# The squares of the queries in two bf16 halves: one more square on ScalarE and one subtraction on GpSimd, summed by TensorE as bf16

## The reference

```python
q = (layernorm(x) @ Wq).reshape(B, 100, 16, 128)
k = (ctx @ Wk).reshape(B, 361, 16, 128)
v = (ctx @ Wv).reshape(B, 361, 16, 128)
q = q * rsqrt(mean(square(q), -1) + 1e-5) * gq
k = k * rsqrt(mean(square(k), -1) + 1e-5) * gk
attn = softmax(einsum('bqhd,bkhd->bhqk', q, k) / sqrt(128), -1)
x = x + tanh(g_xattn) * (einsum('bhqk,bkhd->bqhd', attn, v).reshape(B, 100, 2048) @ Wo)
x = x + tanh(g_ffn) * ffn(layernorm(x))      # ternary weights, activations in 8 bits
```

## Time and profile before

| | |
|---|---|
| median of 3 runs | 2375.84 us (2372.43 to 2377.09) |
| the profiled execution | 2376.88 us, its span 2375.1 us |
| TensorE busy | 2225.2 us, 94% of the span |
| VectorE busy | 1842.7 us, 78% |
| ScalarE busy | 1615.7 us, 68% |
| GpSimd busy | 1283.2 us, 54% |
| granted clock, mean | 0.973 of full |

### The profile page before, as it was taken

The page is one execution under the profiler, slowest core; times in us unless marked ns, Lnnn a source line. Parts: engine busy times, 40 slices in busy tenths (PEclk is TensorE's granted clock), DMA queues, the critical chain, the costliest instruction groups (busy, mean ns, idle before and its releaser), DMA issues. The chain is left out here.

```text
span 2375.1 us, 45246 instructions
## 1 busy us (share of the span) xinstructions
PE 2225.2 (94%) x16338; PEld 1572.4 (66%) x16338; DVE 1842.7 (78%) x4138; ACT 1615.7 (68%) x3374; POOL 1283.2 (54%) x1632
## 2 busy tenths in 40 slices
PE   3599999999999999999999999999999999869999
PEld 1367776777777777777677767676767777534444
DVE  4577878787878787877877888787777877669997
ACT  3567676777777777766776767776767767536665
POOL 4365655565656566665766676766666655300000
PEclk8799999999999999999999999999999999989999
DMA  7456767676767666657676777677767765636655
GB/s 204 104 108 114 142 129 135 128 144 122 148 126 148 124 139 128 132 108 138 130 151 123 146 136 139 138 141 147 136 146 131 137 108 112 149 109 142 139 141 125
DMA packets 919312, 317.50 MB, mean 134 GB/s; under 512 B 864528, under 2 KB 882224, under 8 KB 918832
## 3 DMA queue, kind: packets, MB, share of 16 engines
q1 hardware_dynamic: 919088, 314.60, 65.5%
HBM read 82.09 MB, written 19.40 MB: 43 GB/s over the span
## 5 line engine op out<-in xcount | busy, mean ns | idle before, releaser
L1084 POOL TENSOR_TENSOR ksplit<-khat,ksplit 128x512 bf16<-128x512 f32 (+1 forms) x384 | 454.8, 1186 | 72.3 <-ACT ksplit L615 71.4
L825 DVE TENSOR_TENSOR khat<-keys_ps,krs 128x512 f32<-128x512 f32 (+1 forms) x384 | 263.5, 686 | 279.2 <-POOL krs L1078 278.9
L1078 POOL TENSOR_TENSOR krs<-kvar,minus_half 128x4 f32<-128x4 f32 (+1 forms) x384 | 387.6, 1009 | 32.0
L635 ACT ACTIVATE early<-score_ps,nbias,qrs 100x361 f32<-100x361 f32 x512 | 329.3, 648 | 83.6 <-DVE nbias L843 82.1
L1075 POOL TENSOR_SCALAR kvar<-kss 128x4 f32<-128x4 f32 (+1 forms) x384 | 88.1, 229 | 551.4 <-DVE kss L815 549.4
L620 ACT ACTIVATE ksq<-keys_ps 128x512 f32<-128x512 f32 (+1 forms) x384 | 228.5, 596 | 193.2 <-PE keys_ps L25 193.1
L644 ACT ACTIVATE psplit<-early,rden 100x361 bf16<-100x361 f32 x512 | 304.5, 595 | 61.5 <-DVE rden L849 60.6
L23 PE MATMUL keys_ps<-wk_split,ctxT 128*128 128x512 bf16 (+1 forms) x768 | 296.7, 386 | 38.0 <-DVE khat L825 31.4
L855 DVE SCALAR_TENSOR_TENSOR psplit<-early,rden,psplit 100x361 bf16<-100x361 f32 x512 | 321.8, 637 | 7.1 <-ACT psplit L644 3.3
L833 DVE TENSOR_REDUCE nmax<-score_ps 100x1 f32<-100x361 f32 x512 | 268.5, 525 | 55.8 <-PE score_ps L25 55.6
L615 ACT ACTIVATE ksplit<-khat 128x512 bf16<-128x512 f32 (+1 forms) x384 | 240.7, 627 | 99.7 <-DVE khat L825 86.4
(11 more groups left out here) (136 smaller groups left out, 5331.6 us busy)
## 6 DMA issues: line engine op xcount, KB each, us to landing
w_raw<-in_ffn SPq DMA_DIRECT2D x96, 256.0 KB, 3.3
ctx_raw<-in_ctx SPq DMA_DIRECT2D x31, 256.0 KB, 3.3
xin<-in_x SPq DMA_DIRECT2D x32, 200.0 KB
xres<-in_x SPq DMA_DIRECT2D x32, 200.0 KB
x_rows<-xres SPq DMA_DIRECT2D x32, 200.0 KB
xin<-x_rows SPq DMA_DIRECT2D x25, 256.0 KB, 2.8
xres<-x_rows SPq DMA_DIRECT2D x25, 256.0 KB, 2.9
out<-xres SPq DMA_DIRECT2D x25, 256.0 KB, 2.0
```

The source lines that it names most:

```text
L635: act.activation(prob[:, b, h, :], score_ps[h % 2][0:SQ, 0:SK], ACT.Exp, bias=nbias[:, b, h:h + 1], scale=qrs[:, v // 2 % 2, r:r + 1], acc ...
L825: dve.tensor_tensor(khat[0:KV[t], k, :].rearrange("p (h d) -> p h d", h=G), keys_ps[k][0:KV[t], :].rearrange("p (h d) -> p h d", h=G), rs, ...
L1078: pool.tensor_tensor(krs[0:KV[t], k, :], kvar[0:KV[t], k, :], minus_half[0:KV[t], 0:G], ALU.pow).then_inc(krs_done, 1)
L1084: pool.tensor_tensor(ksplit[0:KV[t], t, 1, :], khat[0:KV[t], (u + t) % 2, :], ksplit[0:KV[t], t, 0, :], ALU.subtract).then_inc(k_lo_done, 1)
```

## The change

`queries_square` now squares each 128x400 block twice from the same PSUM bank: into a float32 tile of half the size (`qsq`, one block), and as bf16 into the high part of `qsq_split`. A new function on GpSimd, `query_squares_lo`, subtracts the one from the other into the low part. As `qsq` holds one block, ScalarE's next square waits for GpSimd's subtraction. `query_squares` waits for GpSimd and makes two bf16 products for each sequence and head; the weights are 128 columns, of which the last 28 belong to the neighbour or to a zeroed pad, and land in rows that nobody reads. `w_ones` moves into a part of `early`, and `yT` into the memory of `qsq_split`.

```diff
-        qsq = sb("qsq", [P, G, QT], F32)
+        qsq, qsq_split = sb("qsq", [P, TWO, QT], F32), sb("qsq_split", [P, 2 * G * QT + PAD], BF16)
...
             def query_squares(i, u):
                 ps = shared_bank(i, ("qss", u))
-                eng.wait_ge(q_sq_done, i * (NG * QD) + ((u + 3) // 2 + 1) * QD)
+                eng.wait_ge(q_sqlo_done, i * (NG * QD) + ((u + 3) // 2 + 1) * QD)
                 for b in range(2):
                     for h in range(G):
-                        last = pe.matmul(ps[0:SQ, b * G + h:b * G + h + 1], qsq[:, h, b * SQ:(b + 1) * SQ],
-                                         ones[:, 0:1], start=True, stop=True)
+                        out, hi, lo = ps[:, b * G + h:b * G + h + 1], h * QT + b * SQ, (G + h) * QT + b * SQ
+                        pe.matmul(out, qsq_split[:, hi:hi + P], ones[:, 0:1], start=True, stop=False)
+                        last = pe.matmul(out, qsq_split[:, lo:lo + P], ones[:, 0:1], start=False, stop=True)
...
             def queries_square(i, u, k):
...
-                act.activation(qsq[:, k * TWO:(k + 1) * TWO, :],
-                               shared_ps[p][:, 0:TWO * QT].rearrange("p (h q) -> p h q", h=TWO),
-                               ACT.Square).then_inc(q_sq_done, 1)
+                if started(i * (NG * QD) + (u + 3) // 2 * QD + k):
+                    eng.wait_ge(q_sqlo_done, i * (NG * QD) + (u + 3) // 2 * QD + k)
+                act.activation(qsq[:, :, :], ps, ACT.Square).then_inc(q_sq_done, 1)
+                act.activation(qsq_hi[:, heads, :], ps, ACT.Square).then_inc(q_sqhi_done, 1)
...
+            def query_squares_lo(i, u, k):
+                heads = slice(k * TWO, (k + 1) * TWO)
+                n = i * (NG * QD) + ((u + 3) // 2 * QD + k + 1)
+                eng.wait_ge(q_sq_done, n)
+                eng.wait_ge(q_sqhi_done, n)
+                pool.tensor_tensor(qsq_lo[:, heads, :], qsq[:, :, :], qsq_hi[:, heads, :],
+                                   ALU.subtract).then_inc(q_sqlo_done, 1)
...
                 if ku:
-                    key_scale(i, u + 2, 1), keys_lo(i, u + 2, 0)
-                    key_scale(i, u + 2, 2), keys_lo(i, u + 2, 1), keys_lo(i, u + 2, 2)
+                    key_scale(i, u + 2, 1)
+                if qu:
+                    query_squares_lo(i, u, 0)
+                if ku:
+                    keys_lo(i, u + 2, 0)
+                    key_scale(i, u + 2, 2), keys_lo(i, u + 2, 1)
+                if qu:
+                    query_squares_lo(i, u, 1)
+                if ku:
+                    keys_lo(i, u + 2, 2)
```

More of the change, by code:

```diff
@@ L47, in attention_block @@
     SQR = -(-SQ // 16) * 16
+    PAD = -(-(P - SQ) // 16) * 16
     NT = DM // P
@@ L175, in attention_block @@
         qT_hi, qT_lo = sb("qT_hi", [P, 2, G, QT], BF16), sb("qT_lo", [P, 2, G, QT], BF16)
-        qsq = sb("qsq", [P, G, QT], F32)
+        qsq, qsq_split = sb("qsq", [P, TWO, QT], F32), sb("qsq_split", [P, 2 * G * QT + PAD], BF16)
+        qsq_hi, qsq_lo = (qsq_split[:, a * G * QT:(a + 1) * G * QT].rearrange("p (h q) -> p h q", h=G)
+                          for a in range(2))
         psplit = sb("psplit", [SQR, QD, 2, TWO, SKF], BF16)
@@ L179, in attention_block @@
         assert NT == G
-        yT = qsq
+        yT = qsq_split[:, 0:2 * G * QT].bitcast(F32).rearrange("p (m q) -> p m q", m=NT)
         xres = sb("xres", [SQ, 2, DM], F32)
@@ L185, in attention_block @@
         w_abs, w_part = sb("w_abs", [P, MATRICES, CHUNKS], F32), sb("w_part", [P, MATRICES], F32)
-        w_ones, w_inv = sb("w_ones", [P, P], F32), sb("w_inv", [P, MATRICES], F32)
-        ident, ones = sb("ident", [P, P], F32), sb("ones", [P, 2], F32)
+        w_ones, w_inv = early[:, 2 * G * SK:2 * G * SK + P], sb("w_inv", [P, MATRICES], F32)
+        ident, ones = sb("ident", [P, P], F32), sb("ones", [P, 2], BF16)
         minus_half, zeros = sb("minus_half", [P, 2 * G], F32), sb("zeros", [P, P], BF16)
@@ L229, in attention_block @@
         q_hi_done, q_sq_done, o_hi_done = sem("q_hi_done"), sem("q_sq_done"), sem("o_hi_done")
+        q_sqhi_done, q_sqlo_done, sq_zero = sem("q_sqhi_done"), sem("q_sqlo_done"), sem("sq_zero")
         qrs_done, y_done, y_free, p_zero = sem("qrs_done"), sem("y_done"), sem("y_free"), sem("p_zero")
         y_turned, y_added = sem("y_turned"), sem("y_added")
-        w_raw_in, w_summed, w_part_done, w_total_done = (
-            sem(n) for n in ("w_raw_in", "w_summed", "w_part_done", "w_total_done"))
+        w_raw_in, w_summed, w_ones_ready, w_part_done, w_total_done = (
+            sem(n) for n in ("w_raw_in", "w_summed", "w_ones_ready", "w_part_done", "w_total_done"))
         w_scale_done, w_inv_done, w_scaled, w_clipped, w_rounded, w_tern_out, w_tern_in = (
@@ L526, in weight_totals @@
             def weight_totals(i):
+                eng.wait_ge(w_ones_ready, 1)
                 eng.wait_ge(w_part_done, 1)
@@ L1118, in round_chunk @@
                 m = tern_chunk_of(i, u)
+                if (i, u) == (SUM_PAIR, 1):
+                    eng.wait_ge(w_lo_done, len(pieces))
+                    pool.memset(w_ones[:, :], 1.0).then_inc(w_ones_ready, 1)
                 if m is not None:
@@ L1163, in two_turns @@
                     split_ctx(i + 1, b, 2, 1 - par, ctx_raw)
-            pool.memset(w_ones[:, :], 1.0).then_inc(consts_ready, 1)
             pool.memset(ident[:, :], 0.0).then_inc(ident_zero, 1)
@@ L1176, in _ @@
             pool.memset(psplit[:, :, :, :, :], 0.0).then_inc(p_zero, 1)
+            pool.memset(qsq_split[:, 2 * G * QT:], 0.0).then_inc(sq_zero, 1)
+            eng.wait_ge(sq_zero, 1)
             eng.wait_ge(p_zero, 2)
-            eng.wait_ge(consts_ready, 5)
-            eng.sem_inc(consts_ready, 1)
+            eng.wait_ge(consts_ready, 4)
+            eng.sem_inc(consts_ready, 2)
             for b, raw in enumerate((ctx_raw, ctx_early)):
@@ L1186, in _ @@
                 key_scale(-1, u, 2), keys_lo(-1, u, 1), keys_lo(-1, u, 2)
-            query_scale(-1, UNITS - 3)
-            query_scale(-1, UNITS - 1)
+            for u in (UNITS - 3, UNITS - 1):
+                query_squares_lo(-1, u, 0), query_squares_lo(-1, u, 1)
+                query_scale(-1, u)
             first_turn(-1, UNITS)
```

1 line of the change is left out of this document (added).

## The result

The change takes **2414.14 us** (median of 4 runs, 2412.76 to 2416.19), the kernel before 2374.14 (4 runs): a ratio of 1.0168, 95% interval 1.015 to 1.0185. The forecast was 2406 us and "slower". The profiled span is 2411.0 us, 35.9 more than before.

What follows compares the result with a forecast made beforehand. TensorE, 94% busy, was taken as the bound, VectorE's chain 0.56 us behind. Losses of 16.0 us (ordinary turns) and 14.1 (x turns) add 30 us to 2376.9; with the median 1 us lower, 2406 us, 8-in-10 range 2357 to 2425.

Steps and rivals of the forecast that it cites:

- What can be won: Ordinary turn: TensorE can start the heads' product at most 0.56 us earlier, since VectorE's second uT low half ends at 1058.82.
- The batch: TensorE's 16 products become bf16 pairs at an estimated 42 ns instead of 84: 0.67 us a batch, 0.68 saved.
- ScalarE: 128 more squares, each putting its queue back 0.40 us; the second key tile's high half moves from 1052.62 to 1053.02.
- GpSimd: 128 more subtractions of 0.94 us; the first pushes VectorE's last khat of the turn by 0.21 us.
- The walk: One ordinary turn: uT's first low half 0.84 us late, heads' product at 1059.45, its second half at 1060.83 against 1060.49.
- The step that was short: One walked ordinary turn taken for all: each loses 0.34 us, 47 of them 16.0 us.
- The x turns: 15 turns that turn x, paced by VectorE throughout: each loses one added subtraction's width, 0.94 us, 14.1 us in all.
- The preamble: Two batches there, where ScalarE and the weight loads set the pace, priced at nothing.
- VectorE wins the race: Rival: the probabilities' low half starts before GpSimd's second subtraction, against a 0.13 us margin; 6 us faster, 2370 us; chance 0.20.
- The holds cost nothing: Rival: GpSimd's new subtractions only push VectorE by 0.21 us; 2363 us, or 2349 without the push; chance 0.20.
- TensorE alone counts: Rival: all 64 batches' savings of 0.68 us become time, 44 us faster, 2332 us; chance 0.02.
- The clock falls too: Rival: shorter batches with waits behind them bring half-clock stretches to ordinary turns, 27 us more, 2433 us; chance 0.08.

Runs made afterwards that it cites:

- TensorE's part alone: Kernel before with only the batch's products changed: bf16 pairs using the high half twice, nothing added on GpSimd or ScalarE; 2362.58 us against 2373.44, ratio 0.9955.
- the fills: The change with each GpSimd subtraction of the squares replaced by two zero fills of its output, at the same places; 2384.13 us, ratio 1.0046.
- the later places: The change with ScalarE's high half copied from SBUF after more urgent work, GpSimd's subtractions one or two key steps later, two float32 blocks; 2377.1 us, ratio 1.0015.
- Two additions: Kernel before plus, into an unused tile, ScalarE's second square (2378.26 us) or GpSimd's two subtractions a turn (2393.82 us); both together 2417.8 us.

## Why the prediction was right, and where it was short

The mechanism was right in the turn that was walked: the added subtraction takes the gain and more, by way of VectorE. That the total of 2406 us came so near was in part luck, since the kinds of turn were off in both directions.

- **What can be won** (0.56 us up to VectorE's chain): right in kind. In the turns that end in u = 7 TensorE's part alone gained 0.46. Wrong for the whole, 11 us and not 47 x 0.56 = 26: u = 1 gained 0.09, and the x turns lost 0.25.
- **The batch** was taken at 42 ns a pair, measured are 25. The reason given, half the bytes in half the time, is shown by no run. As the text said, no price under 49 changes the sum. The trace agrees with the floor of about 25 ns in the Trainium skill (TensorE: Matmul & The Clock Gate, Wait — 56ns, not 53.3ns?).
- **ScalarE**: the shift of 0.40 us onto the high half of the second key tile came as worked out (1073.82 is 1053.01 on the clock of before, forecast 1053.02). That it costs nothing by itself held in ordinary turns. Not foreseen: in the x turns it puts a key subtraction over the layernorm.
- **GpSimd**: one subtraction 0.95 us (forecast 0.94); the krs wait of khat 1.51 in place of 1.34, a push of 0.17 (forecast 0.21).
- **The walk** held to a few hundredths. Less 20.81 us: first low half of uT 1057.14 (forecast 1057.15), second 1058.79 (1058.81), heads' product 1059.49 (1059.45), its second half 1060.80 (1060.83), 0.31 later than before. By TensorE's waits, though, only uT's low half shows as a cause; those for the read of the squared sums fell from 10.1 us to 7.7.
- **The step that was short**: "an ordinary turn loses 0.34 us, and 47 of them lose 16.0". It fits the 15 intervals that end in u = 7, 0.32. Those that end in u = 5 lose 0.02 at the same clock, those that end in u = 1 lose 0.81. 15 x (0.02 + 0.32 + 0.81) = 17 us is near the 16.0 only because the two errors nearly cancel. VectorE's rows of a turn with u = 1, before and now:

```profile
1114.32 0.96 DVE L843 TENSOR_TENSOR nbias<-nmax,qrs 100x1 f32<-100x1 f32 x1
...
1115.28 0.57 DVE L855 SCALAR_TENSOR_TENSOR psplit<-early,rden,psplit 100x361 bf16<-100x361 f32 x1
1115.77 0.15 DVE L843 TENSOR_TENSOR nbias<-nmax,qrs 100x1 f32<-100x1 f32 x1
```

```profile
1136.38 0.39 DVE L852 TENSOR_TENSOR nbias<-nmax,qrs 100x1 f32<-100x1 f32 x1
...
1136.77 1.50 DVE L864 SCALAR_TENSOR_TENSOR psplit<-early,rden,psplit 100x361 bf16<-100x361 f32 x1
1138.18 0.35 DVE L852 TENSOR_TENSOR nbias<-nmax,qrs 100x1 f32<-100x1 f32 x1
```

  Here the two key subtractions and the new one between them run on without a gap; the low half of the probabilities meets the last of them (1136.71 to 1137.87) and takes 1.50 us. TensorE starts the heads' product 1.71 us behind the start of its batch, where it was 1.35: 0.36 us late itself, besides the late second half of the turn before, which falls into the same interval.
- **The x turns**: forecast 0.94 each and 14.1 us in all, measured 0.95 in the mean of the 16 intervals, 15.2 in all. That the width of one added subtraction, 0.94 us, was the right size is luck: two smaller holds and the push make it up. VectorE's rows of such a turn, before and now:

```profile
1021.00 0.56 DVE L881 TENSOR_SCALAR xin<-xin,ln_mv,ln_rstd 100x512 f32<-100x512 f32 x1
...
1022.46 0.32 DVE L843 TENSOR_TENSOR nbias<-nmax,qrs 100x1 f32<-100x1 f32 x1
```

```profile
1039.63 0.69 DVE L834 TENSOR_TENSOR khat<-keys_ps,krs 105x512 f32<-105x512 f32 x1 [1.54 <-POOL krs L1087]
...
1040.67 0.74 DVE L890 TENSOR_SCALAR xin<-xin,ln_mv,ln_rstd 100x512 f32<-100x512 f32 x1
...
1042.32 1.02 DVE L852 TENSOR_TENSOR nbias<-nmax,qrs 100x1 f32<-100x1 f32 x1
```

  That is 0.18 + 0.70 = 0.88 us of holds, besides the push.
- **The preamble** at nothing: the third batch's heads' product came 1.6 us later, the stretch behind the last 1.3 us shorter.
- **The rivals**: *VectorE wins the race* did not happen: the second subtraction starts ahead of the low half in every turn of the trace. The margin in the walked one was 0.14 us (forecast 0.13). *The holds cost nothing* is refuted by the fills and by the later places. *TensorE alone counts*: that experiment gave 2363, not 2332. *The clock falls too* came true in small: 0.971 against 0.973 in the profiles, 10 us more at the low clock, some 4 us of time by the estimate above. The four executions of the change have 0.967 to 0.971, the 13 of before that were measured beside the experiments 0.971 to 0.978. That the waits behind the batch lower the clock isn't shown.
- **From 2406 to 2414**: the forecast added 30 us, the profiles differ by 36. The 6 us are some 3 of clock in the intervals that end in u = 5, 1 of ordinary turns and 1 of x turns. The rest, to the 40 us between the medians, lies in the choice of the two profiled executions.

## What to carry to other kernels

Before work is moved to an engine that has room, look where in its queue it lands, and at which instructions of another engine are kept waiting by it: the same halves cost 52 us more than TensorE's part alone at one set of places and 15 at another. Walk every kind of turn that the kernel has, not one; here the kinds lost from 0.02 us (at the same clock) to 0.95, and an average that comes out right can hide that. Compare turns with the same granted clock before a difference is put down to a change. And ask what stands next behind the bound: a unit that is 94% busy gave 11 us back for the 61 taken off it.

## What the runs showed of the hardware that was not expected

- A fill on GpSimd, which reads nothing, left the bias product and the probabilities' low half alone (means 319 and 632 ns, against 374 and 698 with subtractions) but held a float32 layernorm step with one SBUF input and an SBUF output. It took 1.13 us in place of 0.54, in part for the key subtraction before the fill, and ended 0.28 us behind the fill; behind a key subtraction alone it ended 0.29 us after that (1026.72 and 1026.43 in the run with ScalarE's second square). The Trainium skill (SBUF — State Buffer, Who interferes with whom) counts that operation among those that can take the shared pair for a whole instruction, unlike a two-input one, which contends with reads alone; the runs agree on both.
- Two additions that cost 3 and 19 us apart cost 44 together; 10 of the 22 us between lie in turns at full clock.
